# First layer of a two-layer ViT tower: row statistics behind the attention's residual on ScalarE instead of VectorE

## The reference

```python
h = tok(x)                                     # 32 images, 36 patches + 2 class tokens, 256 features
h = h + attn0(layernorm(h))                    # weights 1 + s + s*s/2, causal, divided by their sum
h = h + ffn0(layernorm(h))                     # 4-bit block quantised activations and weights
h = h + attn1(layernorm(h))                    # softmax attention, 16 heads
h = h + ffn1(layernorm(h))                     # low rank, gelu

def layernorm(x, eps=1e-5):
    m = mean(x); v = var(x)
    return (x - m) / sqrt(v + eps)
```

## Time and profile before

| | |
|---|---|
| median of 3 runs | 276.23 us (275.45 to 279.44) |
| profiled execution | 275.67 us |
| its span, first to last instruction | 273.9 us |
| PE busy | 240.9 us (88%) |
| DVE busy | 176.6 us (64%) |
| ACT busy | 135.0 us (49%) |
| POOL busy | 130.3 us (48%) |
| granted PE clock | full in all slices |

### The profile page before, as it was taken

How to read it: one execution, slowest core, us unless ns; L and a number is a source line. 1 busy time by engine, 2 the same in 40 slices (tenths; PEclk the granted TensorE clock), 3 DMA queues, 4 the chain that set the end, 5 groups by cost and what they waited for, 6 DMA issues and landing times.

```text
span 273.9 us, 8794 instructions
## 1 busy us (share of the span) xinstructions
PE 240.9 (88%) x3644; PEld 189.0 (69%) x3644; DVE 176.6 (64%) x347; ACT 135.0 (49%) x300; POOL 130.3 (48%) x218
## 2 busy tenths in 40 slices
PE   0779989969999899998897999999999997988983
PEld 0667878857787688887686888789988884443331
DVE  0534537621567899999997998898777776435111
ACT  1322011146576566664455566675766554823450
POOL 7331433561042737565587766878654561154000
PEclk9999999999999999999999999999999999999999
DMA  5989650000111011111100000000000000002021
GB/s 165 221 229 304 131 133 0 4 0 30 47 43 35 31 36 38 35 36 36 33 11 0 2 2 2 2 5 6 2 0 2 5 2 0 4 0 68 2 68 45
DMA packets 12541, 12.44 MB, mean 45 GB/s; under 512 B 4435, under 2 KB 11670, under 8 KB 12502
## 3 DMA queue, kind: packets, MB, share of 16 engines
q1 hardware_dynamic: 12086, 11.88, 15.5%
q10 hardware_dynamic: 416, 0.01, 0.1%
HBM read 8.07 MB, written 1.25 MB: 34 GB/s over the span
## 4 chain that ended last, share of the span: by engine, by line
PE 63%; DVE 18%; issue 7%; DMA 5%; ACT 4%; SPq 2%; DVEq 0%; ACTq 0%
PE psum L1261 12%; PE psum L1297 9%; PE psum L1458 5%; PE psum L1441 5%; DMA img<-in_x 4%; PE psum L1541 3%; PE psum L1604 3%; PE psum L1592 3%; DVE img L1024 3%; PE psum L1516 3%; PE psum L1376 2%; PE psum L1531 2%; PE psum L1233 2%; DVE big L1016 2%; PE psum L1574 2%
## 5 line engine op out<-in xcount | busy, mean ns | idle before, releaser
L481 POOL TENSOR_SCALAR ve<-mvs 114x1 f32<-114x1 f32 x44 | 17.0, 387 | 81.1 <-DVE mvs L979 80.2
L1297 PE MATMUL psum<-hnT,a 128*128 128x114 f32 x352 | 49.0, 282 | 1.1 <-issue 0.6
L1297 PEld LDWEIGHTS psum<-hnT,a 128*128 128x128 f32 x352 | 43.1, 191 | 6.7 <-ACT img L702 2.6
L1261 PE MATMUL psum<-wT,patchT 128*114 128x256 f32 x132 | 33.0, 404 | 1.6 <-DVE patchT L933 0.8
L476 POOL TENSOR_SCALAR big<-mT,parmask 128x228 f32<-128x228 f32 x22 | 22.3, 1026 | 18.4 <-ACT mT L671 18.4
L482 POOL TENSOR_TENSOR rstd<-ve,nhalf 114x1 f32<-114x1 f32 x44 | 28.2, 641 | 3.7
L1261 PEld LDWEIGHTS psum<-wT,patchT 128*114 128x114 f32 x132 | 24.3, 190 | 7.0 <-DVE patchT L933 2.1
L1016 DVE SCALAR_TENSOR_TENSOR big<-big,img 76x912 f32<-76x912 f32 x11 | 15.8, 1438 | 13.1 <-ACT big L727 12.9
L977 DVE BATCH_NORM_STATS2 st<-h_all 114x6 f32<-114x256 f32 x44 | 18.8, 428 | 1.5
L1024 DVE RECIPROCAL img<-img 128x228 f32<-128x228 f32 x11 | 17.3, 1570 | 1.0 <-ACT img L736 1.0
L840 ACT ACTIVATE qc<-psum,b 128x456 f32<-128x456 f32 (+1 forms) x24 | 13.1, 609 | 9.1 <-PE psum L1592 9.1
(11 more groups left out here) (154 smaller groups left out, 513.9 us busy)
## 6 DMA issues: line engine op xcount, KB each, us to landing
img<-in_x SPq DMA_DIRECT2D x6, 576.0 KB, 10.5
img<-vS SPq DMA_DIRECT2D x66, 38.0 KB
out<-h_all SPq DMA_DIRECT2D x10, 114.0 KB
w_raw<-in_L_tok_W SPq DMA_DIRECT2D x1, 768.0 KB, 6.1
a_raw<-in_L_attn_Wq SPq DMA_DIRECT2D x1, 256.0 KB, 8.4
a_raw<-in_L_attn_Wk SPq DMA_DIRECT2D x1, 256.0 KB, 8.5
a_raw<-in_L_attn_Wv SPq DMA_DIRECT2D x1, 256.0 KB, 8.8
a_raw<-in_L_attn_Wo SPq DMA_DIRECT2D x1, 256.0 KB, 12.4
```

The source lines that it names most:

```text
L481: step(nc.gpsimd.tensor_scalar(ve[:, t:t + 1], mvs[:, t, 1:2], LN_EPS, None, ALU.add))
L1261: last = nc.tensor.matmul(EB[t % 2][0:T, 0:D], patchT[:, c, FIRST[t]:FIRST[t] + TI, :].rearrange("p b s -> p (b s)"), wT[:, c, :], start=( ...
L1297: return nc.tensor.matmul(bk[:, m * T:(m + 1) * T], w[:, c, m * 128:(m + 1) * 128], hnT[:, c, :], start=(c == 0), stop=(c == DC - 1))
```

## The change

`residual0` on DVE keeps its addition and loses BN_STATS and BN_AGGR. A new function `stats0` on ACT makes two passes over the tile's 256 columns, each with an accumulated output: a Copy scaled by -1/256, which gives minus the mean, and then, behind a wait for that, a Square with minus the mean as bias, which gives the sum of squared deviations. `rstd_0_step` on POOL takes its input from these and waits for the second pass. `stats0(t-1)` takes the place of `ffn_norm(t-1)` in ACT's program, and `ffn_norm(t-1)` moves behind `take_q0`, ahead of `take_hnT0`. In iteration 10 both stand behind the last `take_hnT`, and for tile 10 both stand at the end of the attention's iteration 0.

```diff
@@ POOL
             def rstd_0_step(t):
-                pool.wait_ge(var_ready, NT + t + 1)
-                step(static_rstd(t))
-                nc.gpsimd.tensor_scalar(shift[:, t:t + 1], mvs[:, t, 0:1], rstd[:, t:t + 1], -1.0, ALU.mult, ALU.mult
+                pool.wait_ge(square_0, t + 1)
+                step(nc.gpsimd.tensor_scalar(ve[:, t:t + 1], squares[:, t:t + 1], 1.0 / D, LN_EPS, ALU.mult, ALU.add))
+                step(nc.gpsimd.tensor_tensor(rstd[:, t:t + 1], ve[:, t:t + 1], nhalf[:, :], ALU.pow))
+                nc.gpsimd.tensor_tensor(shift[:, t:t + 1], nmean[:, t:t + 1], rstd[:, t:t + 1], ALU.mult
                                         ).then_inc(rstd_ready, 1)
@@ ACT
+            def stats0(t):
+                act.wait_ge(lay[0]["h"], t + 1)
+                nc.scalar.activation(spread0[:, :], h_all[:, t, :], ACT.Copy, scale=-1.0 / D,
+                                     accum_out=nmean[:, t:t + 1]).then_inc(mean_0, 1)
+                act.wait_ge(mean_0, t + 1)
+                nc.scalar.activation(spread0[:, :], h_all[:, t, :], ACT.Square, bias=nmean[:, t:t + 1],
+                                     accum_out=squares[:, t:t + 1]).then_inc(square_0, 1)
@@ ACT, layer0
                         take_k0(t + 2)
                         if t > 0:
-                            ffn_norm(t - 1)
+                            stats0(t - 1)
                         take_v0(t + 2)
...
                         if i == 0:
-                            ffn_norm(t - 1)
+                            stats0(t - 1)
...
+                    if 0 < t < NT - 1:
+                        ffn_norm(t - 1)
                     if t == NT - 1:
                         take_xT((t - LAG) // 2)
...
                     if t == NT - 1:
+                        stats0(t - 1)
                         ffn_norm(t - 1)
@@ ACT, attention
                     if t == 0:
+                        stats0(NT - 1)
                         ffn_norm(NT - 1)
@@ DVE
             def residual0(t):
                 nc.vector.tensor_tensor(h_all[:, t, :], h_all[:, t, :], YB0[0:T, 0:D], ALU.add).then_inc(L["h"], 1)
-                dve.wait_ge(L["h"], t + 1)
-                static_stats(t, var_ready)
```

More of the change, by code:

```diff
@@ L90, in vit_tower @@
         rstd = sb("rstd", [T, NT])
+        nmean = sb("nmean", [T, NT])
+        squares = sb("squares", [T, NT])
+        spread0 = sb("spread0", [T, D])
         nhalf = sb("nhalf", [T, 1])
@@ L261, in vit_tower @@
         shift_ready = sem("shift_ready")
+        mean_0 = sem("mean_0")
+        square_0 = sem("square_0")
         squared = sem("squared")
@@ L452, in rstd_step @@
             def rstd_step(t):
-                pool.wait_ge(var_ready, 2 * NT + t + 1)
+                pool.wait_ge(var_ready, NT + t + 1)
                 static_rstd(t).then_inc(rstd_ready, 1)
```

## The result

The changed kernel takes 298.27 us (median of 4 runs, 297.47 to 300.11) against 276.32 for the kernel before on the same chip: 1.080 times as long, with an interval of 1.075 to 1.085. Slower was right. The forecast of 284.2 and its range up to 290 were not: the loss is 22 us where 8 were forecast. The profiled execution took 298.34 us, with a span of 296.6.

The account below looks back on a forecast made before the run. PE was taken to bound the kernel as a whole, DVE iterations 4 to 8. Terms 2.3 + 4.95 + 1.1 - 0.4 = 7.95 on 275.67 gave 283.6, plus 0.56 for the median 284.2 us; range 278.5 to 290.

Parts of the forecast that it names:

- the first term: Up to the second layer's first scores: lags in iterations 3 to 9 make `scores(0)` start 2.3 us late.
- the load on ACT: ACT's added passes, in iterations 1 and 2 hidden behind PE's and DVE's work: costed at nothing, up to 0.4 us if uncovered.
- the way back: Even iterations, from the start of `quantised` through PE, ACT and POOL until `scores` can start: 6.25 us, against 5.59 before.
- The other half of the ring: Per pair, from `scales` to `quantised`: 9.2 us; with 6.25 for the rest, 15.45 against 15.13, so 0.3 lost per pair.
- the lag shrink at iteration 9: DVE's lag of 4.0 us shrinks by 0.7 (one more residual) and 1.1 (PE's output projection in hand).
- The handover: Second term, iteration 10: `scores(1)` waits for POOL's expansion of tile 1 behind late statistics: +4.95 us, 4.5 to 5.8 by bounds.
- The odd iteration's first lag: Iteration 3: POOL's rounding stands behind `rstd_0_step`, which waits for ACT, so `quantised` starts 3.0 us late.
- The accumulated output: ACT's passes: giving out the accumulated value taken as 0.20 us per pass, from nothing to 0.60 as upper bound.
- Tile 10: Third term: `stats0(10)` and its `ffn_norm` stand ahead of the attention's `take_m(3)`: +1.1 us; the shorter last residual gives -0.4.
- Not slower: Rival: lags find cover in iterations 3 to 8, 3.3 us come back, first scores do not wait: 272.9 us, chance 0.07.
- Only the handover: Rival: the DVE stretch wins 3.3 us, then 4.95 + 1.1 are lost: 279.0 us, chance 0.17.
- The dear accumulator: Rival: accumulated output costs 0.60 us a pass, `stats0` 0.8 longer, eight times on the path: 290.6 us, chance 0.16.

Follow-up runs that it names:

- bias_gated: Changed kernel, but for the first three pairs POOL's bias addition waits until DVE's `quantised` is done: 293.29 us, 1.061 of the kernel before.
- fill_short: Changed kernel plus unread matmuls on PE: 4 calls before `turn_quantised` in iterations 4, 6, 8 and 8 before `scores(1)`: 290.67 us, 1.053.
- expand_first: Changed kernel, but in POOL's iteration 10 the expansion of tile 1 stands ahead of `rstd_0_step(9)`: 292.88 us, 1.053 of the kernel before.
- passes_only: Kernel before, plus `stats0`'s two passes on ACT with unused results; DVE still makes the statistics: 282.4 us, 1.022.
- no_stats: Kernel before without the first layer's residual statistics on DVE, nothing in their place, so part of the computation is left out: 274.91 us, 0.989.
- both orders: Changed kernel; POOL rounds before `rstd_0_step` in odd iterations from 3, and expands tile 1 before `rstd_0_step(9)`: 282.58 us, 1.023 of the kernel before.
- the hybrid: Kernel before, with `stats0` on ACT for tiles 2, 4, 6 only, their statistics step behind POOL's rounding, their `ffn_norm` behind `take_hnT0`: 278.24 us, 1.004.
- fill: Changed kernel plus unread matmuls on PE: 8 calls before the transposes of `quantised` in iterations 4, 6, 8 and 17 before `scores(1)`: 298.72 us, 1.075.

## Why the prediction was wrong

**What failed: the first term, +2.3, measured at +14, and the load on ACT, put at nothing.** The step that failed is the one on the even iterations, "the way back" from `quantised` to `scales`: 6.25 us forecast, 8.60 measured in the second pair (116.89 to 125.49), 8.50 and 9.73 in the others. The other half of the ring was nearly right: 9.2 forecast, 9.54 and 9.55 measured. Row by row for the second pair:

| part | forecast | measured | from |
|---|---|---|---|
| `quantised` to PE's transposes | 0.60 | 2.33 | 116.89 to 119.22 |
| transposes and keys to `take_k0` | 1.40 | 2.39 | 119.22 to 121.61 |
| `take_k0` | 0.70 | 0.68 | 121.61 to 122.29 |
| `stats0` | 1.35 | 1.14 | 122.29 to 123.43 |
| POOL and hops | 1.45 | 1.43 | 123.43 to 124.86 |
| `ffn_norm` and hop | 0.75 | 0.63 | 124.86 to 125.49 |

The parts that the change added were sized well. The two that were wrong stand at its top, and have three causes:

- **The residual behind `quantised`.** `turn_quantised` also waits for DVE's residual, which stands behind `quantised`. Before, the transposes began 1.27 us after `quantised` did (112.64 on PE, 111.37 on DVE), so 0.6 was wrong there already: 0.67 us per pair that the trace at hand would have given. I had read what `quantised` lasts, not when PE starts.
- **Contention, 1.06 us per pair.** I moved the rounding onto the mask and allowed 0.3 for it, but did not ask what the bias addition behind it would now meet. Before it met the mask (109.22 on POOL, 109.45 on DVE), where its cost was already paid (2.00 against 1.07). Now it meets `quantised`, which was ahead of it before and which PE waits for. The rule that the prediction quoted from the Trainium skill, "SBUF — State Buffer", Who interferes with whom, fits: 0.68 became 1.74, and 1.06 of the 1.26 us of the addition is the wait. `bias_gated` shows it.
- **The clock, 0.99 us in this pair, some 7.6 us in all.** With PE idle for 1.4 to 4.4 us at five places it came back at the lower level, for 3.9 to 6.3 us each, and matmuls took up to twice their time. The prediction took every PE duration from a trace in which the clock stood at 1.00 throughout. `fill_short`, which fills four of the five places, shows the 7.6 as a difference of medians. At a clock of 1.00, in the trace of `expand_first`, the way back takes 7.23 and 7.39 us: the 6.25 of the forecast and the 1.73 of the two causes above, less 0.6 to 0.8 by which the other parts came in under.

Because each feeds the next (a longer `quantised` makes a longer idle time, behind which the clock was lower in this trace, which makes the keys and so `stats0` later), the sum is more than its parts: 6.3 us of lag at `scales(1)` instead of 3.4, then 3.0 and 4.1 more in two pairs, where 0.6 was forecast for both. Nor did the lag shrink at iteration 9, where 0.7 and 1.1 us were to come off it: the 13.5 us at `scales(3)` are 14.0 at `scores(0)`, which waits 1.12 us for POOL's expansion of tile 0.

**Costed at nothing, and not nothing:** ACT's load in iterations 1 to 3. The two passes alone make the kernel 5.5 us slower; of the 6.1 us in the trace of `passes_only` 3.5 lie ahead of keep(0), 1.5 of them before the clock falls. It is PE-bound ground, and I had only asked how full ACT was.

**What was right.** The handover: the order of `stats0`, POOL's step and the expansion behind the last `take_hnT` made PE wait 4.36 us, and `expand_first` took 5.4 us off. Forecast 4.95, measured 6.0, of which 1.2 are the clock (2.62 against 1.44). The odd iteration's first lag: forecast 3.0, measured 3.7 (28.23 against 24.52 from divide(0) to `quantised(0)`). The accumulated output is a short instruction of its own, 0.18 to 0.20 us, as taken from rows 4.

**What came out right by luck.** Tile 10 and what follows it: forecast 1.1 less 0.4, and keep(1) to keep(3) is 1.1 longer. But 0.7 of this is the product behind `scores(1)` at the lower clock (1.53 against 0.86 us), and only 0.4 is PE's wait for ACT (0.64 us, where it idled 0.30 before).

**The rivals.** Not slower: refused by the result, and DVE's whole saving is 3 us by `no_stats`. Only the handover: refused, 14 us are lost ahead of it. The dear accumulator reached 290.6 and would have been nearest in time, but for a wrong reason: the passes were cheaper than forecast. The true case was none of them: the same waits, at a higher price each, and a load that was not free.

**What stays open.** With both orders the kernel is still 6 us behind. In its trace (a span of 281.2 us against 273.9) 4.1 lie before keep(0), where `passes_only` loses 3.5, 1.1 at the handover, 1.0 from there to keep(3), and 0.8 behind; that the first are the same loss as in `passes_only` is likely from the sizes, and not shown. What decides whether the clock falls is not told by these rows: the same issue gap of 1.37 us at the same place brought it down in the changed kernel and in `passes_only`, and not in both orders. In the last stretch of the changed kernel four matmuls took 3.33 us behind an idle time of 1.18, where the kernel before took 1.77 behind one of 1.17. That is 1.6 of the 2.3 us there, and that idle time is no longer than before. And the hybrid's faster pairs do not show in its median; its executions other than the profiled one ran at a lower mean clock, but why is not found.

## What to carry over

When a producer moves to another engine, price first who stands behind it in that engine's order and behind each consumer; here a rounding and an expansion on POOL that stood behind a wait cost 16 of the 22 us. The work itself is not free because its engine is half empty: the two passes alone cost 5.5. Where the change makes PE idle, do not copy PE durations from a trace at full clock: give the range a term for the lower level behind each new gap, since one trace can show it and the next not. And for every instruction that shifts, ask what it now runs beside, on SBUF as well as on the path; and read when a consumer starts, not how long its producer lasts.

## What the runs showed of the hardware

- The clock at work: 48 matmuls that took 1.44 us took 2.62 behind a 4.36 us idle time, and in `passes_only` also 2.62 behind idle times of 1.03 and 0.74 with work between; 8 of the keys 2.01 instead of 1.10 behind 2.10. The five slow stretches lasted 3.9 to 6.3 us. Idle times of 1.37, 1.45, 1.79 and 1.86 us were followed by full speed in other places or other traces.
- An accumulated output on ACT is a second record behind each pass, 0.18 to 0.20 us; the passes over 114x256 took 0.41 (immediates) and 0.51 us (one pointer). The Trainium skill, "ScalarE: Activation LUTs", What ACT_TABLE_LOAD costs, has a formula by which the passes are estimated at 0.40 and 0.49, and the rows agree; the second record it does not price.
- A two-input elementwise instruction on DVE, 0.68 us, took 1.74 beside a POOL addition of 1.26; and POOL's second rounding instruction took 2.02 instead of 1.27 beside DVE's mask.
- An f32 matmul call of 128x256 stands as two records and took about 0.46 us in `fill` (3.72 us for 8 calls).
